# Weight copies for the half tile moved from ScalarE's queue to SyncE's, a GpSimd drain per round, and a new hand-written order

## What is computed

```python
x = x + tanh(g_xattn) * attention(layernorm(x), ctx)      # 16 heads, 77 keys per batch
x = x + tanh(g_ffn) * ffn(layernorm(x))
# ffn, with n = layernorm(x):
top1 = argmax(softmax(n @ gate_w.T))                      # one of 2 experts for each token
routing_output = sum over e of (relu((n if top1 == e else 0) @ w1[e] + b1[e]) @ w2[e] + b2[e])
shared = relu(n @ sw1 + sb1) @ sw2 + sb2
return routing_output + shared                            # hidden size 1024
```

## Time and profile before

| | us |
|---|---|
| median of 3 runs | 352.46 |
| lowest and highest run | 352.29, 353.43 |
| the profiled execution's own time | 350.86 |
| its span, first to last instruction | 349.1 |
| PE busy | 319.1 |
| DVE busy | 230.1 |
| ACT busy | 216.4 |
| POOL busy | 184.4 |

### The profile page before, as it was taken

One profiled execution on the slowest core, in us unless ns is written; L12 is line 12 of the kernel. 1 busy time (PEld: TensorE's weight loads), 2 busy tenths in 40 slices (PEclk: granted clock), 3 DMA queues, 4 the chain that ended last, 5 costly groups with the idle time before them and its releaser, 6 DMA issues.

```text
span 349.1 us, 7274 instructions
## 1 busy us (share of the span) xinstructions
PE 319.1 (91%) x2363; PEld 284.6 (82%) x2363; DVE 230.1 (66%) x516; ACT 216.4 (62%) x483; POOL 184.4 (53%) x261
## 2 busy tenths in 40 slices
PE   7996688999989999999999999964999999999980
PEld 7764557779878788887998899964999999999970
DVE  6999789899989878877847936321344454445370
ACT  2765998869577577579764854442447554755560
POOL 8317989893643485736530775303245434563441
PEclk9999899999999999999999999988999999999995
DMA  6991846636131040431421004095023212321310
GB/s 192 297 327 31 257 103 157 141 95 207 16 94 38 5 118 0 107 105 48 168 74 60 0 17 141 29 366 207 4 86 90 67 25 88 92 60 30 91 46 12
DMA packets 38151, 35.69 MB, mean 102 GB/s; under 512 B 16608, under 2 KB 35060, under 8 KB 37613
## 3 DMA queue, kind: packets, MB, share of 16 engines
q1 hardware_dynamic: 33992, 23.17, 24.2%
q0 software_dynamic: 2720, 7.32, 6.4%
q10 hardware_dynamic: 1413, 4.87, 3.8%
HBM read 21.20 MB, written 9.85 MB: 89 GB/s over the span
## 4 chain that ended last, share of the span: by engine, by line
PE 68%; DVE 11%; DMA 7%; ACT 6%; issue 3%; SPq 2%; POOL 0%; ACTq 0%; DVEq 0%; POOLq 0%
PE y_ps L1535 25%; PE h_ps L1535 18%; PE bank L1535 10%; PE s_ps L1535 9%; DMA x_all<-in_x 5%; PE bank L1668 4%; DMA xs<-sorted_dram 3%; DVE rsum L1264 1%; PE bank L1772 1%; DVE stats L1147 1%; DVE probs L1258 1%; ACT xn L885 1%; DVE smax L1246 1%; PE bank L1705 1%; ACT pT L943 1%
## 5 line engine op out<-in xcount | busy, mean ns | idle before, releaser
L678 POOL TENSOR_TENSOR probs<-probs,rinv 128x616 f32<-128x616 f32 x32 | 41.3, 1294 | 37.2 <-DVE rinv L1268 36.9
L1469 DVE TENSOR_TENSOR hT_lo<-h,hT_hi 128x256 fp32r<-128x256 f32 x64 | 29.6, 463 | 43.4 <-ACT h L1086 43.4
L1535 PE MATMUL y_ps<-ew,hT_hi 128*128 128x256 f32 x256 | 54.3, 290 | 3.0 <-DVE hT_lo L1469 3.0
L1535 PEld LDWEIGHTS y_ps<-ew,hT_hi 128*128 128x128 f32 x256 | 43.4, 194 | 3.2 <-DVE hT_lo L1469 3.2
L1535 PE MATMUL y_ps<-sw_hi,hT_hi 128*128 128x256 f32 x136 | 40.7, 299 | 1.2 <-DVE hT_lo L1513 1.2
L982 ACT ACTIVATE hT_hi<-h_ps,vec_cols 128x512 fp32r<-128x512 f32 (+1 forms) x40 | 24.3, 608 | 24.0 <-PE h_ps L1535 23.6
L1535 PE MATMUL y_ps<-sw_lo,hT_hi 128*128 128x256 f32 x136 | 38.4, 282 | 0.0
L1535 PE MATMUL y_ps<-sw_hi,hT_lo 128*128 128x256 f32 x136 | 38.4, 282 | 0.0
L1083 ACT ACTIVATE hT_hi<-h_ps,vec_cols 128x256 fp32r<-128x256 f32 x32 | 15.2, 475 | 35.1 <-PE h_ps L1535 28.5
L1535 PE MATMUL y_ps<-ew,hT_lo 128*128 128x256 f32 x128 | 36.6, 286 | 0.0
L808 POOL DMA_INDIRECT out<-final,scatter_token x16 | 18.1, 1129 | 30.2 <-issue 30.2
(11 more groups left out here) (214 smaller groups left out, 920.1 us busy)
## 6 DMA issues: line engine op xcount, KB each, us to landing
v_diag<-v_rows SPq DMA_DIRECT2D x16, 256.0 KB
stage<-in_L_ffn_w SPq DMA_DIRECT2D x4, 1024.0 KB, 5.7
xs<-sorted_dram SPq DMA_DIRECT2D x8, 257.0 KB
stage<-in_L_ffn_sw SPq DMA_DIRECT2D x2, 1024.0 KB, 6.7
sw_hi<-ew ACTq DMA_DIRECT2D x2, 1024.0 KB, 5.9
sw_lo<-ew ACTq DMA_DIRECT2D x2, 1024.0 KB, 10.2
x_all<-in_x SPq DMA_DIRECT2D x1, 1536.0 KB, 10.1
part_dram<-x_all SPq DMA_DIRECT2D x3, 512.0 KB, 2.9
```

The lines of the kernel that those rows point to most:

```text
L678: nc.gpsimd.tensor_tensor(pq, pq, rinv[:, b % 2, k, :].unsqueeze(2).to_broadcast([P, HG, KEYS]), ALU.mult).then_inc(p_ready, 1)
L1469: nc.vector.tensor_tensor(hT[1][:, c % HB, 0:RTOK], h32[:, c % 2, 0:RTOK], hT[0][:, c % HB, 0:RTOK], ALU.subtract).then_inc(h_lo, 1)
L1535: return nc.tensor.matmul(out_, lhsT, rhs, start=start, stop=stop, **kw)
```

## The change

- The shared weights become one tile `sw` with four slots, so that a loop counter can address a slot.
- ACT no longer waits for `y_used` and `w_lo` ahead of its rounds, no longer loads `HALF_EXPERT`, and issues no copies.
- SP waits for `w_lo` of the expert weights ahead of its loop. Its loop is split: in rounds 0 to 3, behind each `load_sorted`, it waits for `y_used` and issues one of the four copies.
- POOL drains in every round, between the additions (L802) and the wait for the final sum.
- `LO_ON_POOL` goes from (1, 4, 5) to (4, 5, 7). Four quarters (15, 20, 22, 23) are added to `FOLDED`, which had ten. The bank for the next round's transposes is 0, not 1.
- The five orders are rewritten from the third batch on, with small exchanges before it. `ot.0.0` and `ot.0.1`, which stood in DVE's work on the fourth and fifth batch, stand together behind `val.4.1`. On SP `vz.1` goes behind `kw.1` and `wd.1` ahead of `wd.0`. The last part of the shared network has the transposes of the first sorted rows (`xst`) one chunk later, and chunk 7's low part on POOL.

```diff
-LO_ON_POOL = (1, 4, 5)
-FOLDED = {2, 4, 11, 12, 16, 19, 25, 29, 30, 31}
-SORTED_BANK = 1
+LO_ON_POOL = (4, 5, 7)
+FOLDED = {2, 4, 11, 12, 15, 16, 19, 20, 22, 23, 25, 29, 30, 31}
+SORTED_BANK = 0
...
-    sm.3.3 su.3.2 val.2.1 ss.3.3 dg ot.0.0 hl.0 su.3.3 sm.4.0 inl.6.0 hl.2 x1.2.1 su.4.0 hl.3 s2.1 sm.4.1 ss.4.1
-    ot.0.1 su.4.1 sm.4.2 ss.4.2 inl.7.0 su.4.2 hl.6 ch.0 hl.7 val.3.1 sm.4.3 n2l.1.0.0 su.4.3 n2l.1.1.1 x1.3.0
+    sm.3.3 su.3.2 val.2.1 dg su.3.3 x1.2.1 hl.0 sm.4.0 inl.6.0 hl.1 s2.1 hl.2 ch.0 su.4.0 sm.4.1 hl.3 ss.4.1
+    su.4.1 sm.4.2 inl.7.1 ss.4.2 val.3.0 su.4.2 sm.4.3 x1.3.0 su.4.3 hl.6 sm.5.0 n2l.1.0.0 n2l.1.1.1 su.5.0 hl.8
+    sm.5.1 hl.9 ad.0 ss.5.1 pl.0.1 hl.10 su.5.1 sm.5.2 ch.1 hl.11 su.5.2 sm.5.3 su.5.3 ot.0.0 val.4.1 sm.6.0
...
-        sw1_sb = [sb(f"sw1_{n}", [P, KC, HIDDEN], F32R) for n in ("hi", "lo")]
-        sw2_sb = [sb(f"sw2_{n}", [P, HC, DIM], F32R) for n in ("hi", "lo")]
+        sw = sb("sw", [P, 4, KC * HIDDEN], F32R)
+        sw1_sb = [sw[:, n, :].rearrange("p (k h) -> p k h", k=KC) for n in range(2)]
+        sw2_sb = [sw[:, 2 + n, :].rearrange("p (k d) -> p k d", k=HC) for n in range(2)]
...
-            with sp.Fori(0, rounds - 1) as j:
+            def routed(j):
                 sp.wait_ge(xsT_ps, j + 1)
                 sp.wait_ge(ids_copied, j + 1)
                 load_sorted(j + 1 - again)
+            for n in range(2, 6):
+                sp.wait_ge(w_lo[n], 1)
+            with sp.Fori(0, 4) as j:
+                routed(j)
+                sp.wait_ge(y_used, CHUNKS_SHARED)
+                sp.dma_start(sw[:, bass.ds(j, 1), :].rearrange("p o h -> p (o h)").bitcast(F32),
+                             ew[:, bass.ds(half_expert, 1), bass.ds(j, 1), :].rearrange("p e o h -> p (e o h)").bitcast(F32)
+                             ).then_inc(half_w, 16)
+            with sp.Fori(4, rounds - 1) as j:
+                routed(j)
...
                     nc.gpsimd.tensor_tensor(part[:, t, :], part[:, t, :], other_row[:, 1 - e, :], ALU.add
                                             ).then_inc(part_rdy, 1)
+                pool.drain()
                 pool.wait_ge(seam_rdy, 1)
                 pool.wait_ge(final_rdy, turn)
...
-            half_expert = act.value_load(plan_int[0:1, HALF_EXPERT:HALF_EXPERT + 1], min_val=0, max_val=1)
-            act.wait_ge(y_used, CHUNKS_SHARED)
-            for n in range(2, 6):
-                act.wait_ge(w_lo[n], 1)
-            for n in range(2):
-                act.dma_start(sw1_sb[n][:, :, :].rearrange("p k h -> p (k h)").bitcast(F32),
-                              ew[:, bass.ds(half_expert, 1), n, :].rearrange("p o h -> p (o h)").bitcast(F32)
-                              ).then_inc(half_w, 16)
-                act.dma_start(sw2_sb[n][:, :, :].rearrange("p k d -> p (k d)").bitcast(F32),
-                              ew[:, bass.ds(half_expert, 1), 2 + n, :].rearrange("p o h -> p (o h)").bitcast(F32)
-                              ).then_inc(half_w, 16)
```

More of the change, by code:

```diff
@@ L88 @@
[L88 to L92, removed]
@@ new lines @@
+    h.0.6 ou.3.0 y.0.3 h.0.7 sc.5.0 n2.1.0.0 n2.1.1.1 y.0.4 y.0.5 y.0.6 tn.4.0.0 h.1.0 h.1.1 tn.4.1.1 sc.5.1
+    y.0.7 h.1.2 tn.4.2.0 ct.0.1 h.1.3 sc.5.2 y.1.0 tn.4.3.1 h.1.4 sc.5.3 tn.4.4.0 y.1.1 va.4.1 tn.5.0.0 sc.6.0
+    h.1.5 tn.5.1.0 ou.4.1 y.1.2 h.1.6 sc.6.1 y.1.3 y.1.4 tn.5.2.0 sc.6.2 tn.5.3.1 h.1.7 tn.5.4.0 sc.6.3 ct.1.1
+    y.1.5 va.5.0 sc.7.0 n2.2.0.1 y.1.6 y.1.7 tn.6.0.0 n2.2.1.1 sc.7.1 ou.5.0 ct.2.1 h.2.0 h.2.1 tn.6.1.0 h.2.2
+    sc.7.2 h.2.3 tn.6.2.1 tn.6.3.0 y.2.0 tn.6.4.1 sc.7.3 y.2.1 va.6.0 h.2.4 h.2.5 tn.7.0.1 ou.6.0 y.2.2 y.2.3
@@ L96 @@
+    h.2.6 tn.7.1.1 tn.7.2.0 h.2.7 tn.7.3.1 y.2.4 tn.7.4.0 y.2.5 y.2.6 n2.3.0.1 va.7.0 n2.3.1.1 y.2.7 ct.3.0
+    h.3.0 ou.7.1 h.3.1 h.3.2 y.3.0 h.3.3 y.3.1 h.3.4 h.3.5 y.3.2 y.3.3 h.3.6 h.3.7 y.3.4 y.3.5 n2.4.0.0 ct.4.1
+    y.3.6 y.3.7 h.4.0 h.4.1 oth.1 h.4.2 y.4.0 h.4.3 h.4.4 y.4.1 y.4.2 h.4.5 h.4.6 y.4.3 h.4.7 y.4.4 xst.0 y.4.5
+    y.4.6 y.4.7
 """
 ACT_ORDER = """
-    yte.0 yte.1 wqhi yte.2 vce nm.0 tanh yte.3 ine.0.0 k32.0.0 khi.0.0 wohi k32.0.1 k32.1.0 khi.0.1 q32.0.1
+    yte.0 yte.1 wqhi yte.2 vce nm.0 yte.3 tanh ine.0.0 k32.0.0 khi.0.0 wohi k32.0.1 khi.0.1 k32.1.0 q32.0.1
@@ L104 @@
[L104 to L108, removed]
@@ new lines @@
+    ex.4.0 he.3 te.3.2.1 he.4 te.3.3.0 te.3.4.1 he.5 q32.6.0 ex.4.1 ine.7.1 vae.3.0 ex.4.2 xn2.1 qe.6 he.6
+    ex.4.3 q32.7.1 he.7 n2e.1.0.0 n2e.1.1.1 ex.5.0 te.4.0.0 he.8 he.9 te.4.1.1 he.10 ex.5.1 te.4.2.0 he.11
+    ex.5.2 te.4.3.1 he.12 te.4.4.0 qe.7 ex.5.3 vae.4.1 te.5.0.0 he.13 te.5.1.0 ex.6.0 he.14 ex.6.1 te.5.2.0
+    te.5.3.1 ex.6.2 te.5.4.0 he.15 xn2.2 ex.6.3 vae.5.0 n2e.2.0.1 ex.7.0 te.6.0.0 n2e.2.1.1 ex.7.1 he.16 he.17
+    te.6.1.0 he.18 ex.7.2 te.6.2.1 he.19 te.6.3.0 te.6.4.1 wh.2 ex.7.3 wh.3 vae.6.0 he.20 he.21 te.7.0.1 he.22
@@ L123 @@
[L123 to L126, removed]
+    sm.2.0 su.1.2 ss.2.0 su.1.3 sm.2.1 inl.4.1 ss.2.1 su.2.0 su.2.1 val.0.0 sm.2.2 ss.2.2 x1.0.0 sm.2.3 s2.0
@@ new lines @@
+    wl.1 sm.3.0 su.2.2 inl.5.0 su.2.3 su.3.0 val.1.1 sm.3.1 ss.3.1 x1.1.1 sm.3.2 su.3.1 ss.3.2 wl.0 n2l.0.0.0
+    sm.3.3 su.3.2 val.2.1 dg su.3.3 x1.2.1 hl.0 sm.4.0 inl.6.0 hl.1 s2.1 hl.2 ch.0 su.4.0 sm.4.1 hl.3 ss.4.1
+    su.4.1 sm.4.2 inl.7.1 ss.4.2 val.3.0 su.4.2 sm.4.3 x1.3.0 su.4.3 hl.6 sm.5.0 n2l.1.0.0 n2l.1.1.1 su.5.0 hl.8
+    sm.5.1 hl.9 ad.0 ss.5.1 pl.0.1 hl.10 su.5.1 sm.5.2 ch.1 hl.11 su.5.2 sm.5.3 su.5.3 ot.0.0 val.4.1 sm.6.0
+    ot.0.1 ss.6.0 x1.4.1 su.6.0 sm.6.1 s2.2 hl.14 su.6.1 sm.6.2 ss.6.2 su.6.2 sm.6.3 pl.1.1 ss.6.3 ch.2 sm.7.0
@@ L127 @@
+    val.5.0 n2l.2.0.1 ss.7.0 su.6.3 ad.1 n2l.2.1.1 sm.7.1 x1.5.0 pl.2.1 su.7.0 hl.16 su.7.1 hl.17 sm.7.2 hl.18
+    su.7.2 hl.19 sm.7.3 wl.2 su.7.3 val.6.0 wl.3 x1.6.0 s2.3 hl.22 ot.1.0 ch.3 n2l.3.0.1 ot.1.1 val.7.0
+    n2l.3.1.1 ad.2 pl.3.0 hl.24 x1.7.1 wl.5 hl.25 s2.4 wl.4 hl.26 hl.27 hl.30 ch.4 pl.4.1 n2l.4.0.0 seam ad.3
+    hl.32 hl.33 hl.34 hl.35 hl.38 xsl.0 ad.4
 """
@@ L430, in weights @@
         def weights(n):
-            if n >= 2:
-                return [ew[:, n // 2 - 1, 2 * (n % 2) + m, :] for m in range(2)]
-            return [t[:, :, :].rearrange("p k h -> p (k h)") for t in (sw1_sb, sw2_sb)[n]]
+            own = sw[:, :, :] if n < 2 else ew[:, n // 2 - 1, :, :]
+            return [own[:, 2 * (n % 2) + m, :] for m in range(2)]
         block = ctx.enter_context(nc.Block())
```

40 lines of the change are left out of this document (16 added, 24 removed).

## The result

The changed kernel takes **343.49 us** in the median of four runs (340.09 to 345.53), against 352.38 of the kernel before beside it: ratio 0.971, 95% interval 0.963 to 0.979. Two later measurements of the same kernel gave 0.967 (0.962 to 0.972) and 0.969 (0.964 to 0.973). The forecast was 342.0 us with a range of 338.5 to 347.5, so direction and size were right. The terms behind the sum were not: the drain, taken at nothing, took off 4.3 us, and the rounds with copies, also taken at nothing, lost 3.1 to 4.6 us in the profiled executions. That they cancelled was luck.

What follows compares the result with a forecast made beforehand. PE was taken as the bound, with the first routed round lengthened by ACT's four copies. 350.86 - 9.8 (that round) - 0.7 (DVE's moved steps) = 340.4 us, plus 1.6 to the median: 342.0, range 338.5 to 347.5.

Steps and rivals of the forecast that it cites:

- What bounds the kernel, and the four ACT copies at the seam: PE bounds; ACT's copies delay the first routed round (22.86 us); without them 13.0 us, a gain of 9.8 us.
- SP's register loads: Four loads ahead of `xs` in the first routed round: 0.56 us, then 0.32 each, 1.5 in all instead of 3.8.
- The rival of slow loads: SP's register loads stay slow without the copies' traffic: gain 5.8 us in the first routed round, time 346.0 us; chance 25%.
- PE's idle for `xs`: First routed round: sorted rows issued at 231.0 us, landing at 234.4, so PE waits 1.3 us without a clock fall.
- I take nothing lost, with bounds 0 and 0.9 us for each of four rounds: Rounds 0 to 3, one copy each: a quarter of the traffic delays POOL's gather 0.8 us, within 2.3 us of slack.
- the gather starves behind each copy: Rival: each gather waits for the whole copy, 5.3 us lost in each of four rounds, time 363 us; chance 5%.
- Up to 2.3 us it costs nothing: POOL's drain in each round, between additions and scatter, is covered because the final sum ends 2.3 us behind the additions.
- No row has a drain: The prediction's statement that the profile rows before the change show no drain, given where it weighs the cost of POOL's drain.
- `ot.0.0` and `ot.0.1`, -0.7: Four 0.5 us DVE steps from 90.64 us, moved behind `val.4.1`, remove PE's idle there: at most 0.7 us gained.
- The sum: 350.86 us (profiled execution) less 9.8 for the first routed round and 0.7 for DVE's moved steps: 340.4; median 342.0.
- The prediction's own signs: Wrong if SP's loads near 1 us, DVE waits for POOL in rounds 1-4, or PE idles over 1 us (100-226 us).

## Why the prediction was right, and which of its steps failed

- *What bounds the kernel, and the four ACT copies at the seam:* right. ACT's part, the two idles and the fall of the clock went, and the first round took 12.16 us where 13.0 were forecast. The working took PE's second round at 249.09 from the chain, where its timeline has 248.93; all terms with it are 0.16 us off, which changes nothing.
- *SP's register loads:* right, and now shown. 605 and 273 ns were measured where 560 and 320 were taken, and `xs` was issued 4.64 us behind PE's start where 4.8 were forecast. The rival of slow loads (25%) is out. The floor of about 600 ns for a register load in the Trainium skill's page DMA: Bandwidth & Descriptors (Latency and other measured facts) agrees with the first of SP's four loads (601 to 618 ns outside the traffic) and not with the next ones (260 to 284 ns).
- *PE's idle for `xs`:* 1.3 us was forecast; 0.23 came, and 0.2 to 2.4 us over all executions, none of them near 1.3. The step took one landing time for a quantity that scatters by 2 us.
- *"I take nothing lost, with bounds 0 and 0.9 us for each of four rounds":* **failed**, and it was the term that was too small. The rounds lost 3.1 to 4.6 us in the profiled executions, about the upper end (3.6) and over it; the median of the run without copies does not show it. Two things were wrong in it, and a third stays open. The gather in the first round, issued right behind the copy (at 236.43 and 237.81, the copy at 236.14), was waited for as long under one copy (5.30 us) as it had been under four (5.07), so a quarter of the traffic did not make a quarter of the delay. Over all kernels with the gather right behind a copy this wait was 3.6 to 5.7 us, with the copy moved behind it 3.1 to 3.8, so that not all of it is the copy's. And the chain was followed only to the final sum: a late final sum makes a late scatter, and DVE waits for that with its low parts queued behind (2.49 us at 253.62). Third, this chain reaches only the first two intervals, 2.0 to 2.2 us; what the later ones lose is not explained. The rival *the gather starves behind each copy* had the mechanism of the first round and the wrong size: at most 1.2 us for each of four copies, far from the 2.6 from which it decides.
- *"Up to 2.3 us it costs nothing", and "No row has a drain":* **failed**. The first half is right: in the rounds it costs nothing. But the trace of before did have drains, five of them at the end of the program, and GpSimd's was the longest by far at 4.65 us and the last to end, behind everything that the chain view shows. I looked for what the new instruction costs where it stands, not for what it takes off elsewhere. It gives -4.3 us, some 40% of the gain.
- *`ot.0.0` and `ot.0.1`, -0.7:* the idle at 90 to 100 us went as forecast (9.25 to 10.00 us busy), and the time did not follow. By the medians all that belongs to the orders together is 0 to +1.1 us; its parts were not measured one by one.
- *The sum:* forecast -9.8 - 0.7 = -10.5. By the runs: -6.5 and -4.3, and nothing for the orders, -10.8. The right total from wrong terms that happened to cancel. The prediction's own signs say so too: it called itself wrong if DVE waited for POOL in rounds 1 to 4, and it did (4.02 us), and if PE idled over 1 us in the stage before, and it did (1.86 of the 130.7 us from 100 us on).

## What to carry to other kernels

Read the end of the span like any other stretch, beyond where the chain view stops: a drain that ends last is time in full (4.3 us here). Where GpSimd issues many DMAs, try a drain in a stretch where GpSimd waits anyway. When traffic is spread over rounds, look at what is issued right behind each piece, try the piece behind the small transfer that someone waits for (here the waits became shorter, the time not clearly), and follow a delay through to the transfers it delays in turn.

## What the hardware showed that I had not expected

- GpSimd's drain costs about 82 ns for each DMA that GpSimd has issued since its last drain: 4650, 2827 and 375 ns for 56, 34 and 4, the same to the nanosecond in every kernel of a kind. The Trainium skill's page VectorE: DVE Perf Modes (The DRAIN you can't avoid) calls the drains that the runtime puts into a program's preamble and postamble constant at about 12 ns. Whether those at the end here are of that kind no run shows; they took 375 to 4650 ns on GpSimd and 497 to 499 ns on DVE.
- The first register load on SP takes 982 to 1087 ns with the four copies in flight (385 GB/s of DMA traffic at 228 us in the kernel before) and 601 to 618 without them; the one behind it takes 922 to 973 and 279 to 284.
- **Open.** In all kernels but the one before, ACT starts one hidden chunk in nearly every round late. Two rows of ACT's timeline, first of the kernel before, then of the one without copies:

```profile
266.51 0.47 ACT L1083 ACTIVATE hT_hi<-h_ps,vec_cols 128x256 fp32r<-128x256 f32 x1 [0.57 <-PE h_ps L1535]
```

```profile
259.34 0.47 ACT L1079 ACTIVATE hT_hi<-h_ps,vec_cols 128x256 fp32r<-128x256 f32 x1 [1.82 <-PE h_ps L1531]
```

PE had begun the chunk 0.90 us before the first (265.61) and 2.15 us before the second (257.19), so ACT is 1.25 us late with nothing in the trace that it waits for. It is hidden where there are no copies (rounds of 11.75 us, in the kernel with the drain alone too), and the long rounds have it together with a copy's traffic. How much of the 3.1 to 4.6 us is due to it was not separated; the 0.9 to 2.6 us that the gather can't explain are the room for it. That the kernel with a moved copy still has intervals of 12.5 and 12.1 us points the same way.
